# Attention scores on one core: four of eight channel products added by a DMA in SBUF before the transposes

## The reference

```python
tn = _ln(t, ln1g, ln1b)                       # t: 8 images x 4096 pixels x 64 channels
q2 = (q @ wiq.T + biq).reshape(b, h * w, H, hd)   # H = 8 heads of hd = 8 channels
k2 = (k @ wik.T + bik).reshape(b, h * w, H, hd)
v2 = (v @ wiv.T + biv).reshape(b, h * w, H, hd)
scores = jnp.einsum('inhd,jnhd->nhij', q2, k2) / jnp.sqrt(jnp.float32(hd))
attn = jax.nn.softmax(scores, axis=-1)
z = jnp.einsum('nhij,jnhd->inhd', attn, v2).reshape(b, h * w, c)
```

## Time and profile before

| | |
|---|---|
| Time, median of 3 runs | 1140.54 us (1140.28 to 1140.69) |
| Span of the profiled execution, first to last instruction | 1136.3 us |
| PE busy | 1071.2 us, 94% |
| DVE busy | 1039.7 us, 92% |
| ACT busy | 652.5 us, 57% |
| POOL busy | 510.7 us, 45% |

### The profile page before, as it was taken

How to read it: one execution, slowest core, us unless ns; L and a number is a source line. 1 busy time by engine, 2 the same in 40 slices (tenths; PEclk the granted TensorE clock), 3 DMA queues, 4 the chain that set the end, 5 groups by cost and what they waited for, 6 DMA issues and landing times. The chain is left out here.

```text
span 1136.3 us, 21019 instructions
## 1 busy us (share of the span) xinstructions
PE 1071.2 (94%) x7238; PEld 601.7 (53%) x7238; DVE 1039.7 (92%) x1475; ACT 652.5 (57%) x1525; POOL 510.7 (45%) x422
## 2 busy tenths in 40 slices
PE   4269999999999999999999999999999999999996
PEld 3156787778777777777653333333333333333331
DVE  5459999999999999999988999999999999999996
ACT  4568889888888888888743233253244242342333
POOL 5134564456445544554452424435345344444440
PEclk9999999999999999999999999999999999999998
DMA  8110111111111111110000000030001100030003
GB/s 303 54 37 21 39 29 35 32 39 29 33 35 38 29 31 38 38 29 20 20 20 1 1 1 1 1 75 1 1 1 34 41 1 1 1 74 1 1 1 74
DMA packets 87545, 35.83 MB, mean 32 GB/s; under 512 B 70210, under 2 KB 86851, under 8 KB 86931
## 3 DMA queue, kind: packets, MB, share of 16 engines
q1 hardware_dynamic: 85634, 33.81, 11.1%
q0 software_dynamic: 768, 0.33, 0.2%
q10 hardware_dynamic: 1040, 0.35, 0.1%
HBM read 26.09 MB, written 8.39 MB: 30 GB/s over the span
## 5 line engine op out<-in xcount | busy, mean ns | idle before, releaser
L1173 ACT ACTIVATE y<-banks,cols 128x1024 f32<-128x1024 f32 x96 | 110.3, 1208 | 259.8 <-PE banks L1165 259.8
L900 POOL TENSOR_TENSOR rstd<-var,half 128x8 f32<-128x8 f32 x32 | 80.8, 2526 | 216.5 <-DVE var L755 216.5
L1155 PE MATMUL banks<-mixed_h,cwp 128*128 128x512 f32 x384 | 177.6, 605 | 0.0
L1155 PE MATMUL banks<-early,cwp 128*128 128x512 f32 x372 | 169.2, 602 | 0.5 <-PEq L420 0.5
L1456 POOL TENSOR_TENSOR early<-xs 128x256 f32<-128x256 f32 x95 | 77.1, 811 | 160.1 <-DVE xs L1204 160.1
L1181 DVE TENSOR_TENSOR y<-y,banks 128x512 f32<-128x512 f32 x192 | 119.9, 682 | 15.2 <-ACT y L1173 15.0
L558 PE MATMUL banks<-consts,early 128*128 128x128 f32 x1024 | 133.2, 279 | 0.0
L1189 DVE TENSOR_TENSOR y<-y,banks 128x512 f32<-128x512 f32 x192 | 124.4, 685 | 8.7 <-PE banks L1165 6.5
L577 PE MATMUL banks<-consts,prod 128*128 128x128 f32 x1024 | 128.2, 273 | 2.8 <-DVE prod L526 2.1
L1155 PEld LDWEIGHTS banks<-mixed_h,cwp 128*128 128x128 f32 x384 | 69.0, 189 | 107.9 <-issue 107.9
L558 PEld LDWEIGHTS banks<-consts,early 128*128 128x128 f32 x1024 | 114.3, 144 | 18.8 <-issue 18.1
(11 more groups left out here) (184 smaller groups left out, 1868.8 us busy)
## 6 DMA issues: line engine op xcount, KB each, us to landing
xs<-in_x SPq DMA_DIRECT2D x4, 2048.0 KB, 16.5
xa<-in_x SPq DMA_DIRECT2D x32, 256.0 KB, 2.8
xr<-in_x SPq DMA_DIRECT2D x64, 128.0 KB, 2.8
out_y<-xs SPq DMA_DIRECT2D x32, 256.0 KB, 4.5
cw<-in_L_conv_w POOLq DMA_DIRECT2D x2, 144.0 KB, 3.9
consts<-in_consts ACTq DMA_DIRECT2D x1, 192.0 KB
group<-in_consts SPq DMA_DIRECT2D x1, 64.0 KB
w1n<-in_L_conv_w ACTq DMA_DIRECT2D x1, 64.0 KB
```

What stands on the lines that cost most here:

```text
L900: pool.tensor_tensor(rstd1[:, :], var1[:, :], top["half"][:, :], ALU.pow).then_inc(rstd1_done, 1)
L1155: pe.matmul(psum[PSUM_PAIR[v, q, j]][i][:, :, :], weights(v, i, j).rearrange("p n o -> p (n o)"), mixed[v][i][:, s0:s0 + WIDE, j, :], star ...
L1173: act.activation(pairs(y[i][q][:, :, :]), m1, ACT.Identity, bias=cols[:, (6, 8)[v]:(7, 9)[v]]).then_inc(m1_out[i][q], 1)
```

## The change

The products of part b are stored as one block per part (`prod1[:, b, e, :]`), so that channels 0 to 3 and channels 4 to 7 of a part are each 512 contiguous elements (2 KB) on a partition. A new POOL step, `pool_e_add`, issues for each part one DMA from SBUF to SBUF that adds channels 4 to 7 to channels 0 to 3 in place: 128 partitions x 512 elements, 256 KB, 4 a tile. PE then waits for that DMA (`e_added[b]`) in place of the DVE product, and does 4 transpose-matmuls for a part, 16 for a tile. Part 3's transposes move behind the first two groups of `pe_av`.

```diff
-        prod1 = top["early"][0][:, 0:HD * S].rearrange("p (e s) -> p e s", e=HD)
+        prod1 = top["early"][0][:, 0:HD * S].rearrange("p (b e s) -> p b e s", b=DUOS, e=HD)
...
+        e_added = [sem(f"e_added{b}") for b in range(DUOS)]
...
-            out = prod1[:, :, P * b:P * (b + 1)].rearrange("p e (i j h) -> p i j e h", i=2, j=B)
+            out = prod1[:, b, :, :].rearrange("p e (i j h) -> p i j e h", i=2, j=B)
...
-            wait(pe, p1_dve, DUOS * t + b + 1)
-            for e in range(HD):
-                m = pe.matmul(b2[:, P * b:P * (b + 1)], prod1[:, e, P * b:P * (b + 1)], ident,
-                              start=(e == 0), stop=(e == HD - 1), is_transpose=True)
+            wait(pe, e_added[b], 16 * (t + 1))
+            for e in range(HD // 2):
+                m = pe.matmul(b2[:, P * b:P * (b + 1)], prod1[:, b, e, :], ident,
+                              start=(e == 0), stop=(e == HD // 2 - 1), is_transpose=True)
...
+        def pool_e_add(pool, t, b):
+
+            wait(pool, p1_dve, DUOS * t + b + 1)
+            pool.dma_start(prod1[:, b, 0:HD // 2, :], prod1[:, b, HD // 2:HD, :], accum_op=ALU.add).then_inc(e_added[b], 16)
...
             if tiles[0]:
                 pe_t(pe, t, k)
-            if tiles[2]:
-                pe_scores_t(pe, t - 2, 3)
             if tiles[3]:
                 pe_av(pe, t - 3, 0)
                 pe_av(pe, t - 3, 1)
             if tiles[2]:
+                pe_scores_t(pe, t - 2, 3)
                 pe_scores(pe, t - 2)
...
                 pool_rstd2(pool, t - 4)
             if tiles[1]:
                 pool_bias(pool, t - 1, (k - 1) % RING)
+                pool_e_add(pool, t - 1, 0)
+                pool_e_add(pool, t - 1, 1)
+                pool_e_add(pool, t - 1, 2)
             if tiles[0]:
                 pool_rstd1(pool, t)
+            if tiles[1]:
+                pool_e_add(pool, t - 1, 3)
```

## The result

The changed kernel takes 1211.99 us at the median (1208.25 to 1215.72) against 1140.41 us for the kernel before, run beside it: a ratio of 1.063, interval 1.061 to 1.065, or 71.6 us slower. I had forecast 1172. The sign was right, and the time lies in the range of 1133 to 1214, but the loss is 2.3 times the forecast 31.

What follows compares the result with a forecast made beforehand. DVE was taken to bound right behind PE, at 16.28 us a tile. Removed matmuls 0, layout 0, issues 0 and the DMA wait +31 took the span from 1136.3 to 1167, with 4.2 us more 1172 us; range 1133 to 1214.

Steps and rivals of the forecast that it cites:

- The sign: Whole kernel: the change was forecast to make it slower, chance 0.79, against 0.14 for faster.
- PE's lead of 2%: Attention block: DVE is the next bound behind PE, so removed matmuls gain at most 0.38 us a tile, 11 us.
- Layout and issue cost: DVE's `prod1` writes and POOL's four DMA issues a tile, 0.75 us each: both taken to add 0.
- POOL's issue is dear: Rival on POOL: describing an adding DMA costs 1.3 us an issue, +48 us, 1189 us; chance 0.10.
- The landing time: From start of a DMA's issue to PE's release: taken as 3.5 us, bounds 2.2 to 5.5, hidden up to 2.5.
- just over the edge: Rival on the DMA wait: landing of 2.5 to 2.8 us, 0 to +9 us, 1145 us; chance 0.12.
- The loop through part 3: Part 3's issue through the maximum to the next issue: sets a period of 13.75 us plus landing, 17.25 against 16.28.
- Part 2 is a parallel path of nearly equal length: Part 2's DMA, then about 3.3 us of PE work before part 3: sets the same time, adds nothing.
- do not help: Part 3's loop: halved matmuls do not shorten it; 4 are in series where 8 were, and these were covered before.
- A second term: Wait for part 3's DMA: 1.0 us more a tile in 31 periods, +31 us.
- Faster: Rival on the DMA wait: landing under 2.5 us, DVE sets the period, about 1131 us; chance 0.15.
- slow adding: Rival on the DMA: adding below copy rate, landing 4.4 to 5.5 us and more, +59 to +93 us; chance 0.18.

Runs made afterwards that it cites:

- e4: Kernel before with channels 4 to 7 left out of the scores, 16 transposes a tile, no DMA: 1128.76 us, ratio 0.990.
- e2: Kernel before with the new layout and the adding DMAs issued into a scratch buffer, all 32 transposes kept, PE not waiting for them: 1140.32 us, ratio 1.0003.
- e9: Changed kernel with 4 overwritten filler transposes before the DMA wait in parts 1 and 2 only: 1193.34 us, ratio 1.047.
- e12: Kernel before with only parts 0 and 1 by adding DMA, parts 2 and 3 and the order kept: 1142.9 us, ratio 1.004.
- e10: Changed kernel with channels 6 and 7 left out, so each DMA adds 128 KB where it was 256: 1188.4 us, ratio 1.044.
- e11: Kernel before with parts 0 to 2 by adding DMA, part 3 and its place kept; a repeat run for a readable profile: 1187.76 us, ratio 1.044.
- e3: Kernel before with only part 3's transposes moved behind the first two groups of `pe_av`, no DMA: 1168.04 us, ratio 1.024.
- e7: Kernel before with only part 0 by adding DMA, 4 transposes a tile less, other parts and order kept: 1131.65 us, ratio 0.993.
- e1: Changed kernel with 4 overwritten filler transposes on PE before every wait for a DMA: 1199.64 us, ratio 1.053.

## Why the prediction was right in direction and wrong in size

**PE's lead of 2%.** Right. DVE's 0.38 us idle time was to be all that the removed matmuls are worth, 0 to 11 us; e4 measured 11.4, and 0.40 a period.

**Layout and issue cost.** Right at 0, by e2. The issue took 0.88 us where I took 0.75, inside the 1.1 us of cover; the second normalization's idle time fell from 1.10 to about 0.2 us. The rival in which POOL's issue is dear is out.

**The landing time.** Taken as 3.5, measured 3.3 / 3.4 / 4.5 (minimum, median, maximum). The Trainium skill (DMA: Bandwidth & Descriptors, "Anatomy of one DMA") has 2.0 us plus bytes over 436 KB per us. The line through the two median landings here, 2.7 us at 128 KB and 3.4 at 256, has a constant of 2.0 too, but 183 KB per us, 2.4 times slower in the part that grows. So the constant agrees and the rate does not, and the estimate of 2.6 us, by which the rival "just over the edge" would have come, is not what these DMAs do. Whether it is the adding or the way from SBUF to SBUF that costs the rate is not shown; no run has a plain copy.

**The loop through part 3.** Right at full clock in its length: 13.75 + 3.5 = 17.25 forecast, 17.23 measured as the shortest of the changed kernel. That it fits to 0.02 us is in part luck. The 11.53 us from the maximum to the next issue of part 3 are as forecast. From that issue to part 3's transposes it takes 3.71 us (553.09 to 556.80), not 3.5, and PE does not wait for the DMA there: it landed by 556.5, and PE's own way from part 2 ended 0.3 us later. From the transposes to the maximum it takes 1.99 us, not 2.23. The two errors cancel. The two paths are nearly equal, as I had worked out, but part 2's is the one that ends last.

**The step that failed** is this one: "Part 2 is a parallel path of nearly equal length", and of its PE work "about 3.3 us", "so it adds nothing now". At full clock that work is 3.41 us. But I had read the granted clock of 1.00 as given, and PE's waits ahead of this path stand in the sum at nothing; the clock is in no term and no rival. The change puts up to 1.6 us of waiting ahead of exactly this path. Where the clock fell behind it, the same work took 6.15 us, and since the path sets the time of the maximum, DVE paid every tenth. That is 30 of the 73 us by the periods, 26.7 of them on this very way, and 18.6 us come back in e9. I even wrote that half the matmuls "do not help", but not that an engine taken off the bound can become it again at half speed.

**A second term was mis-sized.** I charged 1.0 us in each of 31 periods, from one landing time. The landing varies, so that the mean at full clock is 17.52: 1.24 for 1.0, 33.5 us in 27 periods for 27. In four of the 12 full-clock periods (17.61 to 18.10 us) part 3's DMA lands late and PE waits 0.16 to 0.65 us for it; in two (17.69 and 17.81) part 2's transposes start 3.79 and 3.91 us behind the issue for 3.34. Lead-in and end took 9.8 us where I counted 4. In e12 the same spread turns a forecast gain into a loss.

**The rivals.** Faster had been bound to a landing under 2.5 us; even with 128 KB it is 2.7. The range held the time only because slow adding, which did not occur, had widened it to 1214.

The clock's mechanism has one gap. Behind the lead-in the clock falls only in kernels in which PE waits for DMAs: in 15 of 27 periods of the changed kernel, 10 in e10, 9 in e11, 2 in e12, none in the kernel before, e2, e3, e4 and e7. Work put into the waits raises it: e1 and e9 have 2 such periods each. What decides in which period it falls was not found. The periods at 382.68 and 550.27 have the same work and nearly the same waits and read 0.83 and 1.00; the one at 495.71 has a wait of 1.54 us and reads 1.00. Why the landing itself varies was not tried either.

## What to carry to other kernels

Before moving work from a busy engine to a DMA, count for each transfer the time from when its data are ready to when they are wanted, and take only those for which it exceeds the landing with room for the spread. Here one of four nearly did (4.0 us in e7 against 3.3 at the median and 5.2 at most), and it alone pays. A wait on the matrix engine can cost more than its length, because the matmuls behind it may run at half clock: ask whether those are on the path. The order of a software pipeline is part of the price: the same move cost 28 us without the DMA and saved 14 with it.

## What the runs showed of the hardware

- An adding DMA within SBUF, 128 partitions x 2 KB, issued from POOL: 0.88 us of issue on POOL, landing 3.4 us at the median (3.3 to 4.5; up to 5.2 in e2 and e7); with 1 KB a partition 2.7 us. In e2, 128 of them beside a tight pipeline changed the time by 0.1 us.
- In the changed kernel, where PE waits 0.2 to 1.8 us before DMAs once to three times a period and is otherwise nearly always busy (17.87 of 20.50 us), 15 of 27 periods have a stretch at the 1.2 GHz level: granted clock 0.51 over 5.8 us, and 16 matmuls in 3.36 us for 1.97. Single waits do not decide it: periods with waits of 1.54 and 1.84 us kept clock 1.00, and one with waits of 1.11 and 0.34 read 0.83. In e7 a wait of 1.28 us left it at 1.00.
- Filler matmuls that are thrown away made the kernel 12 and 18.6 us faster than the changed one.
